# Leaving out the two idle matmuls of each front slot in a fused four-layer cross-attention and feed-forward kernel

## What is computed

```python
x = x + L0_xattn(layernorm(x), ctx);  x = x + L0_ffn(layernorm(x))   # 6 blocks of local attention and gated ffn
x = x + L1_xattn(layernorm(x), ctx);  x = x + L1_ffn(layernorm(x))   # 16 heads of 8; ffn: fp8-quantised linear
x = x + L2_xattn(layernorm(x), ctx);  x = x + L2_ffn(layernorm(x))   # ffn: shared expert and top 2 of 8
x = x + L3_xattn(layernorm(x), ctx);  x = x + L3_ffn(layernorm(x))   # ffn: top 2 of 8 experts
return x
```

## Time and profile before

| | us |
|---|---|
| median of three runs | 2570.82 (2570.54 to 2572.94) |
| profiled execution | 2574.15 |
| its span, first to last instruction | 2572.4 |
| PE busy over the span | 2402.7 (93%) |
| mean granted clock over the span | 0.975 |

### The profile page before, as it was taken

The page is one execution under the profiler, slowest core; times in us unless marked ns, Lnnn a source line. Parts: engine busy times, 40 slices in busy tenths (PEclk is TensorE's granted clock), DMA queues, the critical chain, the costliest instruction groups (busy, mean ns, idle before and its releaser), DMA issues.

```text
span 2572.4 us, 61077 instructions
## 1 busy us (share of the span) xinstructions
PE 2402.7 (93%) x25528; PEld 1452.4 (56%) x25528; DVE 1905.8 (74%) x3472; ACT 1463.0 (57%) x2051; POOL 1178.8 (46%) x867
## 2 busy tenths in 40 slices
PE   6887899999999999999999999977789999999999
PEld 5775566665666666566666566644444455554443
DVE  4765899999899999999999989935666666454322
ACT  2332566666666666666666666623356677665443
POOL 1221777767777777777776767711111111111000
PEclk9998999999999999999999999988899999999999
DMA  3000000100000000000000100002000001021111
GB/s 120 5 5 5 1 2 2 33 4 12 18 18 7 7 26 10 7 7 26 10 13 2 34 2 10 2 1 83 7 31 14 30 16 39 28 64 50 37 38 41
DMA packets 36006, 55.95 MB, mean 22 GB/s; under 512 B 6365, under 2 KB 20710, under 8 KB 35498
## 3 DMA queue, kind: packets, MB, share of 16 engines
q1 hardware_dynamic: 35754, 52.33, 6.6%
HBM read 51.13 MB, written 1.19 MB: 20 GB/s over the span
## 4 chain that ended last, share of the span: by engine, by line
PE 52%; DVE 25%; ACT 11%; issue 9%; POOL 3%; SPq 0%; DMA 0%; DVEq 0%; POOLq 0%; ACTq 0%
PE w L1402 9%; PE w L1412 8%; DVE turned L1056 4%; DVE norm L1063 4%; PE w L765 4%; PE w L790 4%; PE w L778 4%; PE py L803 4%; PE w L519 3%; DVE straight_odd L1051 2%; DVE top L568 2%; PE w L856 2%; ACT sq L1002 2%; PE w L1531 2%; ACT sq L993 2%
## 5 line engine op out<-in xcount | busy, mean ns | idle before, releaser
L593 POOL TENSOR_TENSOR prob<-prob,rden 128x1024 f32<-128x1024 f32 x112 | 213.2, 1904 | 207.5 <-DVE rden L582 207.5
L563 ACT ACTIVATE prob<-logit 128x512 f32<-128x512 f32 x224 | 137.6, 630 | 282.2 <-DVE logit L571 282.2
L1402 PE MATMUL w<-qT,m_fc 128*128 128x512 f32 x544 | 270.3, 609 | 0.0
L1172 POOL TENSOR_TENSOR straight_odd<-straight_odd,turned 128x1024 f32<-128x1024 f32 x96 | 227.3, 2368 | 82.8 <-DVE turned L1056 79.9
L1172 POOL TENSOR_TENSOR straight<-straight,turned 128x1024 f32<-128x1024 f32 x96 | 226.5, 2368 | 45.0 <-DVE turned L1056 45.0
L1056 DVE TENSOR_TENSOR turned<-w,rot 128x512 f32<-128x512 f32 x384 | 245.6, 681 | 0.0
L1166 POOL TENSOR_TENSOR straight_odd<-straight_odd,rnorms 128x1024 f32<-128x1024 f32 x96 | 180.6, 1902 | 116.9 <-DVE rnorms L1077 116.9
L1063 DVE TENSOR_REDUCE norm<-sq 128x16 f32<-128x1024 f32 x192 | 224.3, 1211 | 0.0
L1166 POOL TENSOR_TENSOR straight<-straight,rnorms 128x1024 f32<-128x1024 f32 x96 | 180.5, 1900 | 72.4 <-DVE rnorms L1077 72.4
L611 POOL TENSOR_TENSOR fresh_roots<-fresh_means,eps 128x1 f32<-128x1 f32 x64 | 12.1, 190 | 401.2 <-DVE fresh_means L600 401.2
L765 PE MATMUL w<-b_wqkv,m_proj 128*128 128x512 f32 x384 | 192.8, 625 | 2.8 <-DVE turned L1056 1.5
(11 more groups left out here) (259 smaller groups left out, 5270.0 us busy)
## 6 DMA issues: line engine op xcount, KB each, us to landing
b_wqkv<-gates SPq DMA_DIRECT2D x64, 256.0 KB, 3.7
b_wqkv<-in_b_wqkv SPq DMA_DIRECT2D x18, 512.0 KB, 3.6
ctxT<-in_ctxT SPq DMA_DIRECT2D x64, 64.0 KB, 1.8
b_wo<-in_b_wo SPq DMA_DIRECT2D x6, 512.0 KB, 3.9
m_fc<-in_m_fc SPq DMA_DIRECT2D x1, 2304.0 KB, 9.1
m_proj<-in_m_proj SPq DMA_DIRECT2D x1, 2304.0 KB, 13.0
m_fc<-in_m_fc SPq DMA_DIRECT2D x8, 256.0 KB, 3.5
m_proj<-in_m_proj SPq DMA_DIRECT2D x8, 256.0 KB, 3.8
```

The source lines that it names most:

```text
L593: pool.tensor_tensor(flat, flat, k.rden[:, s, :, None].broadcast_to([P, HEADS, SEQ]), ALU.mult).then_inc(k.prob_ready, 1)
L1172: pool.tensor_tensor(k.straights[s][:, i, :, :], k.straights[s][:, i, :, :], k.turned[:, i, :, :], ALU.add).then_inc(added, 1)
L1402: pe.matmul(claim(("hidden", J, c)), k.m_fc[:, x, c * P:(c + 1) * P], k.m_xT[:, q, :], start=True, stop=True).then_inc(k.ring_full, 1)
```

## The change

The function `occupy`, its two calls in `front_slot` and the list `claimed` are taken out. 15 front slots, so 30 matmuls (60 passes) and their weight loads go. Nothing else on TensorE moves, and nothing at all on the other engines.

```diff
 def merged_tensor(pe, k):
     d = k.d
     acc = k.w2[:, 0:512]
-    claimed = []
 
     def claim(use):
         r, bank, prior = USES[use]
-        claimed.append(r)
...
-    def occupy():
-
-        if claimed:
-            pe.wait_ge(k.ring_read, claimed[-1] + 1)
-        pe.matmul(k.w2[:, 512:1024], k.ident[:, :], k.s_w[:, 0, :, :].rearrange("p a n -> p (a n)"),
-                  start=True, stop=True)
-
     def front_slot(u, work, before, before2):
...
         if work:
             values(work[0], work[2], u)
             queries(work[0], work[2])
-        occupy()
         if before2:
             turn_rows(before2[2], u)
         if before:
             turn_probs(before[2])
         if before2:
             rows(before2[0], before2[2], u)
-        occupy()
```

## The result

The changed kernel takes 2579.65 us (median; 2577.99 to 2584.99), the kernel before 2572.94 us in the same comparison (2570.54 to 2574.54). The ratio is 1.0031, 95% interval 1.0020 to 1.0042. By the ratio that is about 8 us slower, by the two medians 6.7; predicted were +7.4 us and 2578.2 us, in a range of 2570 to 2583. The profiled execution took 2581.16 us, its span is 2579.4 us, 7.0 more than before.

The account below looks back on a forecast made before the run. The prediction took a dependency loop from one addition to the next as the front's bound. 3.7 + 1.5 + 1.0 + 0 - 0.3 + 1.5 = +7.4 us on 2570.82 gave 2578.2 us, range 2570 to 2583.

Parts of the forecast that it names:

- What bounds the front: Front slots: a dependency loop from addition to addition sets the pace, 9.02 us at full clock, 10.11 at clock 0.84.
- The gap of 3.8 us: PE's pause before `turn_rows` grows from 2.09 to 3.8 us, after which every slot turns its probabilities at half clock.
- Ten ordinary intervals: Front intervals between additions without quantisation: all go to 10.11 us, 97.37 to 101.10 together, +3.7 us.
- Two quantising intervals: The two front intervals with a quantisation: probabilities turned at half clock, +1.08 and +0.44, together +1.5 us.
- Half clock throughout: Front slots staying at half clock: PE's branch comes last by 0.22 us a slot, in somewhat under half, +1.0 us.
- The beginning: Start of the front: up to 4.06 us saved on the chain, up to 5.3 lost to half clock; taken as 0.
- The end and the first expert slot: Last idle matmul ahead of `turn_quad`: -0.3 us; PE work at 1892.34 to 1896.38 possibly at low clock: +1.5 of 4.0.
- The idle matmuls' own time: All 30 idle matmuls on PE: 60 passes of 595 ns at full clock, 36 us at the least.
- (a): Rival: the clock goes as before, only bits of beginning and end gained, -0.3 to -1.5, about 2570 us; chance 0.20.
- (b): Rival: clock stays up through the first three slots, beginning and end gained in full, -5.4, 2565.4 us; chance 0.08.
- (c): Rival: half clock throughout, PE's branch sets every front slot, +12.8, 2583.6 us; chance 0.12.

Follow-up runs that it names:

- its repeat: The changed kernel run once more with no edit, timed against the kernel before: 2580.08 us, ratio 1.0035.
- the kernel with the first only: Against the kernel before, only the idle matmul behind the output projection removed, the one behind `queries` kept in each front slot: 2575.42 us, ratio 1.0010.

## Why the prediction was right, point by point

- *What bounds the front.* Right. In after the loop from addition to addition is 6.57 us to the exponential, which was 6.56, then 1.06, 1.97 and 0.44.
- *The gap of 3.8 us.* Right: 3.81. That every slot would be at half clock behind it: 13 of 14. But the pause was 3 to 4 us in five of 13 slots only and 0.9 to 2.9 in the others, since a run at half clock ends later; all but slot 2 of them turned at half clock as well, so the prediction had the outcome right there and the reason too narrow.
- *Ten ordinary intervals, +3.7.* They went from 97.37 to 100.72 (138.26 less 18.77 twice), +3.35. Two of them, 9.71 and 9.96, got their clock back partway through the transposes.
- *Two quantising intervals, +1.5.* They went to 18.77 both: +2.0. The first lost 1.56, more than the 1.08 of the turn, since behind the wait the run over PE, all at half clock, came last there too. The wait for the quantisation, 4.9 and 5.6 us in before, was said to be in both kernels; it is 6.51 us twice in after, since the idle matmul in front of it is gone.
- *Half clock throughout, +1.0.* Mis-sized. It was put at a little under half of the slots; one ordinary interval shows it (10.31), and the 0.5 just named. It measured about 0.7 in all, which is within the two lines above already: the three terms together were 6.2 predicted and 5.3 measured.
- *The beginning, 0.* Measured -0.7 in after, +0.4 at the other end of the runs without idle matmuls there. That the ends nearly cancel was right; in after `turn_probs` of slot 1 took 1.97 and the run behind it started at half clock.
- *The end and the first expert slot, -0.3 and +1.5.* Mis-sized: the seam measured +4.3 in after and +4.2 in its repeat, where the two terms gave +1.2. The step that was mis-sized is "somewhat under half" of the bound of 4.0: in both profiles the stretch up to slot 15's scores was at 0.50 throughout, which cost 3.4 us, and another 0.9 us was lost behind the stretch that the bound was taken from. The reason given, that PE is less busy there by the 1.36 us of the idle matmul, was right in direction: putting that one matmul back brought 4.5 us of the seam back in the profile.
- *The sum,* +7.4, came out at +8.9 on the same parts of the profiles, at 8 by the ratio and at 6.7 in the medians; the third term was too large, the last too small. That the total came so near is in part luck: the two terms of the seam were 3.1 us too small, and the beginning (0.7 less) and the three interval terms together (0.9 less) made up about half of it. The profiled execution, 2581.16 us against the 2581.6 forecast, is nearer still by luck alone, since -4.1 and +2.2 us of its difference lie in code that both kernels share. The profile of before reached the front at 1734.8 us, later than all others (1729.3 to 1734.2); the 3.3 us by which it was slower than the median need no worse clock in its front, which the prediction had left open.
- *The idle matmuls' own time.* "36 us at the least" counts each pass with 595 ns, but the two passes of one overlap: 1.02 us a pair, 30.6 us for all. No term of the sum rests on it.
- *Rivals.* (a) fell with the intervals and (b) with the beginning. (c), half clock throughout, is what the clock of 0.66 excludes: most ordinary slots got it back behind the transposes, and transposes count.

The forecast signs asked for a mean clock below 0.75 (0.66), transposes at about 1.97 (thirteen of them at 1.56 to 1.97), a gap of 3 to 4 us (3.81 at the first, 0.9 to 3.8 over all), no interval of 9.02 (none), and 10.0 to 10.3 for each (two were 9.71 and 9.96). It was also to count as wrong if the loss sat behind 1890 us. Nearly half of it does: 4.3 of the 8.9 us are the seam's. So the forecast of the front is borne out by itself (+5.3), and the weight given to what follows was too small.

## What to carry to other kernels

An instruction whose result nobody reads may be what keeps TensorE's clock up, so before taking idle work out look at the pause that it fills and at what stands on the loop behind that pause. And where a dependency loop has a piece of TensorE work behind a pause (here 2.1 us went either way, 1.24 was harmless), try idle matmuls in the pause, as many as end before the awaited signal when the engine runs at full clock. One in the pause was worth 5.2 us of the twelve intervals, one beside it 2.2 (133.05 and 136.04 against 138.26 with none), and where the engine entered the stretch at half clock three of them held up the slot. The place to look next is every seam and every wait where TensorE is the full engine behind it: there the time at half clock stands on the path.

## What was not expected of the hardware

Fp32 transposes kept the clock as well as matmuls of the same busy time (twelve intervals 133.15 and 132.92 us, mean clock 0.85 and 0.84). And behind a slot at half clock a single idle matmul at the seam, of 1.35 us, decided over the clock of the whole stretch up to slot 15's scores: 0.97 with it, 0.50 without (after, its repeat, and the kernel with the first only). Behind a slot at full clock that stretch was at 0.65 and at 1.00 without one. Why so little work is enough there is open.
